# A feature-interaction kernel: DVE's sum over relu1 at the end of the step, and a 13th tile of layer 1 in two parts

## What is computed

```
e  = stack of 32 gathered rows                      # (1024, 32, 64)
z0 = einsum('bhd,bmd->bhmd', e, e)                  # 32*32 = 1024 rows
o0 = relu(W0 @ z0 + b0)                             # 128 maps; 64 go on as h, 64 are summed
z1 = einsum('bhd,bmd->bhmd', h, e)                  # 64*32 = 2048 rows
o1 = relu(W1 @ z1 + b1)                             # 128 maps, all summed
feat = sums over the 64 dims of o0[64:], o1         # 192 features
y = relu(relu([feat, dense] @ Wt1 + bt1) @ Wt2 + bt2) @ Wt3
```

## Time and profile before

| | us |
|---|---|
| median of 3 runs | 2170.9 (2169.59 to 2172.28) |
| the profiled execution, its own time | 2169.86 |
| its span in the trace | 2168.0 |
| PE busy | 2065.0 (95%) |
| DVE busy | 1785.7 (82%) |
| POOL busy | 1723.6 (79%) |
| ACT busy | 1556.8 (72%) |

### The profile page before, as it was taken

The page is one execution under the profiler, slowest core; times in us unless marked ns, Lnnn a source line. Parts: engine busy times, 40 slices in busy tenths (PEclk is TensorE's granted clock), DMA queues, the critical chain, the costliest instruction groups (busy, mean ns, idle before and its releaser), DMA issues.

```text
span 2168.0 us, 27494 instructions
## 1 busy us (share of the span) xinstructions
PE 2065.0 (95%) x6856; PEld 1271.6 (59%) x6856; DVE 1785.7 (82%) x1227; ACT 1556.8 (72%) x1814; POOL 1723.6 (79%) x708
## 2 busy tenths in 40 slices
PE   3999999999999999999999999999999999999998
PEld 1565665665665665665665665665665665665663
DVE  3888888888888888888888888888888888888871
ACT  3777777777777777777777777777777777777762
POOL 3888888888888888888888888888888888888761
PEclk9999999999999999999999999999999999999999
DMA  7987876877877876876876877877877876876720
GB/s 191 215 191 163 187 171 161 188 171 162 187 171 161 188 174 158 188 170 162 189 172 160 187 170 162 188 172 161 187 172 161 187 174 160 187 174 159 185 53 0
DMA packets 268303, 364.11 MB, mean 168 GB/s; under 512 B 107505, under 2 KB 107889, under 8 KB 268162
## 3 DMA queue, kind: packets, MB, share of 16 engines
q1 hardware_dynamic: 258338, 352.61, 71.5%
q0 software_dynamic: 8192, 8.40, 1.5%
q10 hardware_dynamic: 1760, 2.96, 0.5%
HBM read 347.02 MB, written 16.78 MB: 168 GB/s over the span
## 4 chain that ended last, share of the span: by engine, by line
PE 62%; DVE 20%; issue 11%; ACT 4%; DVEq 1%; SPq 1%; DMA 1%; POOL 1%; ACTq 0%
PE out L622 48%; PE out L613 12%; DVE prod L559 10%; DVE prod L564 7%; ACT relu L379 4%; DVE z L561 2%; DVE feat L523 1%; POOL zl L218 0%; SPq L260 0%; PE out L671 0%; DMA fields_dram<-emb 0%; PE hrep L671 0%; DVEq L523 0%; SPq L285 0%; SPq L270 0%
## 5 line engine op out<-in xcount | busy, mean ns | idle before, releaser
L218 POOL TENSOR_TENSOR zl<-prod,zh 128x2048 fp32r<-128x2048 f32 (+1 forms) x384 | 1469.5, 3843 | 271.4 <-ACT zh L373 220.9
L373 ACT ACTIVATE zh<-prod 128x2048 fp32r<-128x2048 f32 (+1 forms) x384 | 624.3, 1626 | 199.3 <-DVE prod L559 158.8
L622 PE MATMUL out<-zh,w1h 128*128 128x512 f32 x1536 | 651.0, 424 | 4.3 <-POOL zl L218 4.3
L622 PE MATMUL out<-zl,w1h 128*128 128x512 f32 x1536 | 599.1, 390 | 0.0
L622 PE MATMUL out<-zh,w1l 128*128 128x512 f32 x1536 | 597.9, 389 | 0.0
L613 PE MATMUL out<-prod,w_sb 128*128 128x512 f32 x1024 | 508.9, 620 | 57.7 <-DVE prod L564 35.1
L386 ACT ACTIVATE hrep<-out,b_sb 32x512 f32<-32x512 f32 (+1 forms) x768 | 494.1, 643 | 15.1 <-PE out L608 5.3
L606 PE MATMUL out<-prod,w_sb 128*128 128x512 f32 x1024 | 465.2, 597 | 35.6 <-DVE prod L495 30.7
L613 PEld LDWEIGHTS out<-prod,w_sb 128*128 128x128 f32 x1024 | 174.1, 189 | 367.0 <-DVE prod L564 140.5
L622 PEld LDWEIGHTS out<-zh,w1h 128*128 128x128 f32 x1536 | 288.5, 188 | 91.6 <-issue 30.5
L622 PEld LDWEIGHTS out<-zh,w1l 128*128 128x128 f32 x1536 | 288.7, 188 | 86.9 <-issue 30.4
(11 more groups left out here) (52 smaller groups left out, 862.3 us busy)
## 6 DMA issues: line engine op xcount, KB each, us to landing
rot_low<-fields_dram SPq DMA_DIRECT2D x512, 256.0 KB
rot_high<-fields_dram SPq DMA_DIRECT2D x512, 256.0 KB
xrep<-fields_dram SPq DMA_DIRECT2D x256, 128.0 KB
fields_dram<-emb SPq DMA_DIRECT2D x512, 32.0 KB
left_x<-fields_dram SPq DMA_DIRECT2D x256, 64.0 KB, 3.8
left_y<-fields_dram SPq DMA_DIRECT2D x256, 64.0 KB, 2.3
emb<-in_tables,idx POOLq DMA_INDIRECT x256
w_sb<-in_w ACTq DMA_DIRECT2D x1, 1024.0 KB
```

The costliest lines, as they stand in the source:

```text
L218: pool.tensor_tensor(zl[u][:, :, :], product[:, 0:SIZES[u], :], zh[u][:, :, :].bitcast(F32), ALU.subtract).then_inc(zl_made[u], 1)
L373: act.activation(zh[u][:, :, :], product, ACT.Copy).then_inc(zh_made[u], 1)
L622: mm = nc.tensor.matmul(out1[:, :], w[:, k, :], z[:, t, :], start=False, stop=stop and t == SIZES[u] - 1 and part == 2)
```

## The change

`SIZES` goes from (4, 4, 2, 2) to (4, 4, 3, 2): the third tile of prod[3] is split as well, so ACT rounds and POOL subtracts three tiles of it, PE does nine split matmuls of it and one whole tile. Buffers `zh[2]`, `zl[2]` and the split weights grow by one tile. In DVE's step, `sum_l1(m - 1)` goes from behind prod[2] to behind prod4. z4 gets a wait of its own for part 3's subtraction of the step before, which DVE itself has done.

```diff
-SPLITS = (tiles(P1, 0, 4), tiles(P2, 0, 4), tiles(P3, 0, 2), tiles(P4, 0, 2))
-SIZES = (4, 4, 2, 2)
-FIRST = (0, 4, 8, 10)
+SPLITS = (tiles(P1, 0, 4), tiles(P2, 0, 4), tiles(P3, 0, 3), tiles(P4, 0, 2))
+SIZES = (4, 4, 3, 2)
+FIRST = (0, 4, 8, 11)
 NSPLIT = sum(SIZES)
-WHOLE3, WHOLE4 = tiles(P3, 2, 4), tiles(P4, 2, 4)
+WHOLE3, WHOLE4 = tiles(P3, 3, 4), tiles(P4, 2, 4)
...
                 nc.vector.tensor_tensor(prod[2][:, :, :], repeated(hrep[0], LOW), high[:, :, :],
                                         ALU.mult).then_inc(p2_made, 1)
-                if later:
-                    sum_l1(m - 1)
                 dve.wait_ge(hrep1_made, m + 1)
                 if later:
                     dve.wait_ge(zl_made[2], m)
                     dve.wait_ge(whole3_used, m)
                 nc.vector.tensor_tensor(prod[3][:, :, :], repeated(hrep[1], LOW), high[:, :, :],
                                         ALU.mult).then_inc(p3_made, 1)
+                if later:
+                    dve.wait_ge(zl_made[3], m)
                 nc.vector.tensor_tensor(z4[:, :, :], repeated(hrep[1], 2), low[:, 0:2, :], ALU.mult).then_inc(z4_made, 1)
                 if later:
                     dve.wait_ge(whole4_used, m)
                 nc.vector.tensor_tensor(prod4[:, :, :], repeated(hrep[1], 2), low[:, 2:4, :],
                                         ALU.mult).then_inc(p4_made, 1)
+                if later:
+                    sum_l1(m - 1)
...
             def whole(tiles, product, used, start):
-                for t in range(2):
+                for t in range(tiles.stop - tiles.start):
...
-                whole(WHOLE3, prod[3][:, 2:4, :], whole3_used, True)
+                whole(WHOLE3, prod[3][:, 3:4, :], whole3_used, True)
```

## The result

The changed kernel takes 2061.1 us (2060.4 to 2061.99, 4 runs) against 2171.56 before (4 runs of both on the same chip): ratio 0.9493, 95% interval 0.9476 to 0.9509. The forecast was 2064 us.

A forecast was written before the change was run, and what follows sets the result against it. A ring of waits through relu1 and DVE's sum set 16.26 us a step; POOL binds next at 15.43. Span falls 107.1 to 2060.9, plus 1.9 around it and 1.0 for the median: 2064 us, range 2050 to 2100.

The forecast's parts named there:

- The ring: Chain of waits in the kernel before: splits, relu1, DVE's sum, third product, z4, prod4, four whole-tile matmuls; 16.24 us a round.
- the place of the sum: Behind prod4 on DVE the sum should cost 0.69 us and no wait, relu1 being 1 to 2 us old.
- PE's own round: PE's work per round without waits for DVE: 15.40 us with 12 split tiles, 15.23 with the 13th.
- 0.84 us of stops: PE's waits for DVE's products each round: 0.29 us before the first whole tile, 0.55 before prod4's matmuls; both should go.
- POOL as the new bound: POOL's subtractions, gathers and index addition take 30.87 us a pair of rounds, 15.43 a round, above PE's 15.23.
- The second estimate: Other count of the span: 126 x 16.26 becomes 120 x 15.43 + 6 x 15.23, 105.8 less, 2062.2 us.
- The splits' end: PE's last split matmuls end at about 2023.9 us, before at 2131.0, so the span falls by 107.1 to 2060.9.
- The tight ring: Rival, 16%: ring from POOL's third subtraction through splits, relu1, rounding and subtractions, 14.4 us, binds with little slack; 2100 us.
- The long way: Ring through next but one layer 0, both h copies, first product, its rounding: 29.3 us over two rounds, not binding.
- the reorder frees little: Rival, 8%: the third product finds another late input, PE keeps its waits, only 0.17 us is gained; about 2149 us.
- a third tile costs nothing: Rival, 6%: POOL subtracts three tiles in 2.40 us, its round is 14.35, PE's 15.23 binds; 2040 us.
- a busier DVE would hold POOL: Rival, 4%: POOL's subtractions held once a step for a DVE product of 2.28 us, POOL's round 17.7; 2338 us.

The follow-up runs named there:

- the kernel with the sum alone: Against the changed kernel, 12 split tiles again, the sum kept behind prod4: 2044.86 us, ratio 0.942.
- the two fastest kernels: Changed kernel with POOL subtracting only two tiles of the third product, 2023.44 us; changed kernel with POOL's row-number addition before the odd step's subtractions, 2024.95 us.
- row numbers early: Against the changed kernel, POOL's addition of row numbers issued before the odd step's three subtractions, not behind: 2024.95 us; with 12 split tiles 2044.75, with 14 2168.31.

## Why the prediction was right

**The ring, and the place of the sum.** Right. The chain of the kernel before named the stations, and the two kernels that change one part each confirm them from both sides: without the sum in it the ring is gone (2044.9), and with the sum in it each split matmul counts (2258.4). DVE's time at the new place has no wait, as was said: relu1 is over 1 us before the sum starts.

**PE's own round.** 15.40 with 12 tiles was 0.10 too much, and 15.23 with 13 was 0.11 too much: 15.30 and 15.12 measured. I had taken 0.84 us of stops off the round and left the rest, PE's turns between kinds of matmul, as its own. In the chain of the kernel with the sum alone the turns cost nothing. Where the 0.10 sat shows when both kernels are measured between the same marks. The second split matmul of a round in the kernel before:

```profile
1016.18 0.39 PE L622 MATMUL out<-zh,w1l 128*128 128x512 f32 x1
```

The whole tiles and the second split matmul in the kernel with the sum alone:

```profile
1017.06 3.59 PE L615 MATMUL out<-prod,w_sb 128*128 128x512 f32 x8
...
1020.73 0.39 PE L624 MATMUL out<-zh,w1l 128*128 128x512 f32 x1
```

From the first whole tile to the second split matmul, 4.31 us before (from 1011.87) have become 3.67. So the stop ahead of prod4 cost 0.64 us, not 0.55; the one ahead of the first whole tile cost 0.30 (3.96 from the start of layer 0 for 3.66), close to the 0.29 read. Together they are the 0.94 by which that round of 16.24 exceeds 15.30. In the forecast this counted only in the last six rounds, since POOL was the bound. In the question which part of the change brings what, it decides: on 15.40 the order alone would have given 2063 and the tile nothing either way, and in fact the tile costs 16 us in this kernel. The prediction said that most of what PE could gain from the tile is lost to POOL; it did not say that more than that is lost.

**POOL as the new bound.** Right, and this is the term that carried the number: 15.43 said, 15.42 measured; POOL busy 29.2 us of a pair of rounds, as said; three tiles 3.48 said from the middle of 2.40 and 4.56, 3.52 measured; rounding 1.48 said, 1.47 measured. The second estimate, 120 x 15.43 + 6 x 15.23, comes out as 120 x 15.42 + 6 x 15.12. The splits' end was put at 2023.9; the last sum starts at 2023.47 in the trace, so they end at about 2022.7. From the end of POOL's rounds with gathers that is 93.9 us, as said, which is partly luck: six rounds of 15.23 are 0.7 us too much, so the terms for the end were as much too small. Of the 3 us between 2064 and 2061.1, 1.2 are in the span (2060.9 said, 2059.7 measured) and 1.4 in the median, for which I had added 1.0 to the profiled run and which this time lies 0.4 below it.

**The tight ring** did not bind at 13 tiles: POOL waits for ACT only 13 times, and what PE loses to POOL in every second round (15.67 for 15.12) is the 0.6 us by which two rounds of POOL's exceed two of PE's. The run with 14 tiles shows that it is there, and its size. The long way, put at 29.3 us over two rounds, was not tested by itself; it cannot be longer than the 30.24 that the two fastest kernels take for two rounds.

**The rivals.** That the reorder frees little and that a third tile costs nothing are out by the same rows. That a busier DVE would hold POOL (the broader warning of the Trainium skill, Perfetto Trace Analysis) did not happen: with DVE busy 87% for 82%, the four-tile subtraction takes 4583 ns for 4563. The narrower rule of the Trainium skill (SBUF — State Buffer, Who interferes with whom) agrees with that; it was not put to the test, since no run here has a DVE instruction with two SBUF inputs in the loop.

**The corner that was not asked for.** All times together, in us:

| split tiles | sum behind prod[2] | sum behind prod4 | and row numbers early |
|---|---|---|---|
| 12 | 2170.7 | 2044.9 | 2044.8 |
| 13 | 2258.4 | 2061.1 | 2025.0 |
| 14 | not run | not run | 2168.3 |

The 13th tile costs 88, costs 16 or saves 20 us, by what bounds the kernel around it: the ring through relu1, POOL's total, or PE.

## What to carry to other kernels

In an engine's queue, look at each instruction that waits and ask who needs what stands behind it; a reduction that only the end of the program needs belongs behind the products that the matmuls need now. Then count the next bound as a total with its gaps (gathers, waits for an instruction's own result), not as busy time, since at the bound such gaps cost in full and just below it nothing. A part of a change should be priced against the kernel that has the other parts, because the same tile was a loss under two bounds and a gain under the third.

## What the runs showed beyond the expected

Two stops that were read as 0.84 us, from a recorded start plus the matmuls' spacing, were worth 0.94 in that round and 16.26 - 15.30 = 0.96 on average. Whether PE takes up its work more slowly after a stop, or the recorded starts lie differently after one, is not shown; measuring a kernel with the stop and one without it between the same two marks avoids the question. And a dependent pair on POOL is dear: the addition of the row numbers is 0.2 us long, but the gather that needs it starts 0.8 us after its end. Hidden behind other work, 0.6 of these 0.8 us came off each of 60 pairs of rounds, 36 us in all, before PE's own round stopped it.
